# A macaron transformer layer on one core: masks in VectorE's maxima pass, low halves on GpSimd, half projections one step later

## The chip, the core and the metric

The program runs on one core of one Trainium2 chip. The metric is device time in microseconds (us), the median of several runs. TensorE (PE in the profile) multiplies matrices, VectorE (DVE), ScalarE (ACT) and GpSimd (POOL) work on elements, and SyncE (SP) issues the DMAs. Each engine has a queue of its own, run in order; between engines there are only semaphores.

## The reference, cut to what matters

32 samples of 512 tokens, width 256, 16 heads of 16, two of eight experts for each sample:

```python
x = x + 0.5 * ffn(layernorm(x))          # two experts of the sample, GELU
x = x + attention(layernorm(x))
x = x + 0.5 * ffn(layernorm(x))

# attention
q = cos * q + rotate_half(q) * sin
k = cos * k + rotate_half(k) * sin
scores = einsum('bhqd,bhkd->bhqk', q, k) / math.sqrt(DH)
scores = where(causal, scores, -inf)
out = einsum('bhqk,bhkd->bhqd', softmax(scores), v)
out = out.transpose(0, 2, 1, 3).reshape(b, t, d) @ Wo.T
```

## The kernel before

Three phases: feed-forward over all samples, attention over all samples, feed-forward again. The change is in attention, which fills the stretch from about 427 to 1900 us. Matrices are split into a high and a low half-precision part, so that a product takes three matmuls (`TERMS`).

**Slots and steps.** A sample s has four slots g = 0 to 3, one for each group of four heads; slots are counted through as G. Each slot has up to eleven steps n = 0 to 10. The order of every engine's work in a slot is written out by hand in that engine's `slot(s, g)`, and the queues follow it word for word.

**Work of a slot on TensorE.** At each step n it computes two things: with `scores` the transposed scores of the group two slots back (G - 2), with `max_scores` the scores of the present group, which serve only to find the maximum of each row. The first uses one half of the 128 rows of the array, the second the other half. Steps 0 to 3 of the maxima are one head's last 128 queries against all 512 keys, steps 4 to 7 one head against 384 keys, 8 and 9 two heads against 256, and 10 four heads against 128. Maxima scores go into three banks in turn (`MX_BANK`); a step waits until VectorE has read the bank. Scores go into two banks in turn; a step waits until ScalarE's exponential two steps back is done.

**The causal mask of the maxima.** In steps 0 to 3 VectorE adds the table `over` (f32, zero or -1e30) and takes the maximum in one custom pass (L996), followed by a read of its accumulator. In steps 4 to 10 TensorE adds the mask by one more matmul (L1167) and VectorE reduces (L1006).

**Rotation of the next sample.** In slots 0 and 1 TensorE projects q (tiles t = 0, 1) and k (t = 2, 3) of sample s + 1, each tile in two halves at steps 0, 1 and 4, 5. In slot 2 it projects v at the same steps. VectorE multiplies by the cosine (L974) and swaps neighbours (L975); GpSimd multiplies by the sine (L920, into `by_sin`) and adds (L924, into `rotated`, two buffers). ScalarE rounds to the high half (L1079, slots 1 and 2, steps 0 and 2), VectorE subtracts to get the low half (`rope_low`, L981, slots 1 and 2, steps 0 and 3: t = 0, 1 and t = 2, 3). Its semaphore is `qk_lo`.

**SP.** For sample s + 1: in slot 1 it waits for two low halves and writes the q image to memory (L879, two DMAs). In slot 2 it waits until that has landed, reads it back into the stacks in six DMAs (L846), waits for all four low halves and writes the k image (L888, two DMAs). In slot 3 it waits until this has landed, reads it into the stacks in six DMAs (L846) and waits until all twelve have landed. At the head of every slot it also waits for the negated maxima of the slot before and copies them into the stacks (L862); scores need them two slots later. `max_scores` at step 0 of slot 0 waits for both stacks.

**GpSimd.** In every slot it masks the exponentials of G - 2 with four selects (L912): the first behind exponential 4, two behind exponential 8, one behind 10. Between them stand the rotation of slots 0 and 1, and in slot 2 the power and the normalisation (L942, L948) of sample s + 2, for which TensorE's transposes at step 0 of slot 3 wait. The probabilities' products of the next slot wait for the masks.

```python
            if group(G - 2):
                pool.wait_ge(exp_done, 10 * (G - 2) + 4)
                mask(G, 0, probs[:, 0:4, 0:P], (4,))
            if g < 2 and sample(s + 1):
                rope(s + 1, 2 * g)
```

## Time and profile before

| what | us |
|---|---|
| median of 3 runs | 2292.76 |
| lowest, highest | 2287.46, 2299.47 |
| profiled execution, its own time | 2291.23 |
| its span, first to last instruction | 2289.5 |
| TensorE busy | 2109.5 (92%) |
| VectorE busy | 1931.8 (84%) |
| ScalarE busy | 1354.4 (59%) |
| GpSimd busy | 1306.6 (57%) |

The profile is one execution; its busy shares are means over three phases. In the attention phase the pattern of a sample repeats 32 times, so one sample of it, taken from the middle of the run (1017.8 to 1062.8 us), can be read instruction by instruction. A line such as L996 is a line of the kernel before; the granted TensorE clock is 0.989 of full speed over the span.

### The profile page before, as it was taken

What the parts mean: (1) busy time and instruction counts of PE and PEld (TensorE: products, weight loads), DVE (VectorE), ACT (ScalarE), POOL (GpSimd) and SP (SyncE); (2) the same over time, 40 slices, a digit from 0 to 9 for tenths busy, and PEclk for the clock granted to TensorE, in tenths of its full rate; (3) what the DMA queues carried; (4) which work ended last, traced back from release to release, by engine and by line L of the source; (5) the groups of instructions that cost most, each with busy time, mean ns of one, the idle gap of its engine ahead of it and who ended that gap; (6) DMA issues with size and microseconds to landing.
All of it is one profiled execution on the core that took longest, in us unless ns stands there. A gap on an engine that the chain in (4) does not pass through costs nothing.

```text
span 2289.5 us, 52899 instructions
## 1 busy us (share of the span) xinstructions
PE 2109.5 (92%) x17682; PEld 1141.4 (50%) x17682; DVE 1931.8 (84%) x4485; ACT 1354.4 (59%) x2568; POOL 1306.6 (57%) x1462
## 2 busy tenths in 40 slices
PE   4999999889999999999999999999999888999999
PEld 2666666434444444444444444444444434666666
DVE  6777788788999899999989998999999865777776
ACT  3455444266667666666666676666666655445553
POOL 6666667454555455456545554554555425666664
PEclk9999999899999999999999999999999999999999
DMA  6656666444445444444444454444445423666665
GB/s 208 192 192 207 201 203 200 116 89 89 98 95 101 94 94 98 89 94 93 99 89 100 95 101 94 96 92 96 93 94 98 99 70 118 197 202 194 204 207 167
DMA packets 280391, 295.29 MB, mean 129 GB/s; under 512 B 45784, under 2 KB 263224, under 8 KB 280120
## 3 DMA queue, kind: packets, MB, share of 16 engines
q1 hardware_dynamic: 280120, 291.90, 50.3%
q8 instruction: 143, 2.34, 0.5%
q14 instruction: 128, 1.05, 0.2%
HBM read 140.08 MB, written 83.89 MB: 98 GB/s over the span
## 4 chain that ended last, share of the span: by engine, by line
PE 45%; DVE 33%; SPq 7%; issue 6%; DMA 5%; ACT 4%; DVEq 0%; ACTq 0%
PE bank L710 8%; DVE bank L996 7%; DVE at_mx L1006 7%; PE bank L728 7%; PE bank L1185 6%; PE bank L1202 6%; PE bank L1219 4%; PE bank L1280 4%; ACT probs L1073 3%; DVE turned L975 3%; DVE v_qk L981 3%; DVE turned L974 2%; DVE at_stats L107 2%; PE bank L1255 2%; PE bank L1167 2%
## 5 line engine op out<-in xcount | busy, mean ns | idle before, releaser
L1073 ACT ACTIVATE probs<-bank 128x512 f32<-128x512 f32 x1280 | 747.0, 603 | 456.9 <-PE bank L1185 447.5
L912 POOL TENSOR_SCALAR_AFFINE_SELECT probs<-probs 128x512 f32<-128x512 f32 x512 | 320.4, 638 | 661.1 <-ACT probs L1073 659.3
L1006 DVE TENSOR_REDUCE at_mx<-bank 128x1 f32<-128x384 f32 (+2 forms) x896 | 509.6, 608 | 78.5 <-PE bank L1167 77.0
L1185 PE MATMUL bank<-stacks 49*128 49x512 f16 (+3 forms) x2048 | 458.7, 302 | 71.4 <-ACT probs L1073 71.0
L996 DVE CUSTOM_DVE_ANT_0 bank<-bank,xn 128x512 f32<-128x512 f32 x512 | 351.6, 698 | 38.8 <-PE bank L1158 36.2
L1185 PEld LDWEIGHTS bank<-stacks 49*128 49x128 f16 x2048 | 136.0, 94 | 458.6 <-ACT probs L1073 334.2
L1162 PE MATMUL bank<-stacks 48*128 48x384 f16 (+2 forms) x1536 | 307.7, 275 | 22.1 <-DVE at_mx L1006 15.6
L1167 PE MATMUL bank<-mask,turn 64*128 64x128 bf16 (+2 forms) x896 | 230.7, 257 | 0.0
L1158 PE MATMUL bank<-stacks 48*128 48x512 f16 x512 | 198.5, 389 | 10.6 <-DVE at_mx L996 6.4
L924 POOL TENSOR_TENSOR turned<-turned 128x512 f32<-128x512 f32 x128 | 184.7, 1443 | 19.1 <-POOL turned L920 0.4
L628 ACT ACTIVATE turned<-bank,b1s 128x512 f32<-128x512 f32 x128 | 88.2, 689 | 181.0 <-PE bank L710 179.3
L920 POOL TENSOR_TENSOR turned<-turned,at_sin 128x512 f32<-128x512 f32 x128 | 178.8, 1397 | 27.7 <-DVE turned L975 27.7
L628 ACT ACTIVATE probs<-bank,b1s 128x512 f32<-128x512 f32 x128 | 88.1, 688 | 178.9 <-PE bank L710 177.3
L710 PE MATMUL bank<-stacks 128*128 128x512 f16 x768 | 172.9, 382 | 19.3 <-DVE stacks L568 15.5
L728 PE MATMUL bank<-stacks,v_qk 128*128 128x256 f16 x1536 | 172.7, 273 | 0.0
L1202 PE MATMUL bank<-probs,v_qk 128*32 128x512 f32 (+3 forms) x2048 | 168.6, 448 | 0.0
L1202 PE MATMUL bank<-probs,v 128*32 128x512 f32 (+3 forms) x2048 | 164.3, 439 | 0.0
L728 PEld LDWEIGHTS bank<-stacks,v_qk 128*128 128x128 f16 x1536 | 150.3, 98 | 17.3
L1162 PEld LDWEIGHTS bank<-stacks 48*128 48x128 f16 x1536 | 110.7, 94 | 52.5 <-DVE at_mx L1006 27.0
L710 PEld LDWEIGHTS bank<-stacks 128*128 128x128 f16 x768 | 73.9, 98 | 108.9 <-DVE stacks L568 19.1
L483 POOL TENSOR_TENSOR f_rstd<-f_ve,minus_half 128x4 f32<-128x4 f32 x64 | 91.1, 1424 | 59.4 <-DVE f_ve L119 59.4
L710 PE MATMUL bank<-xThi,w1hi 128*128 128x512 f16 x256 | 99.1, 387 | 25.2 <-DVE xTlo L568 10.6
(145 smaller groups left out, 4619.6 us busy)
## 6 DMA issues: line engine op xcount, KB each, us to landing
stacks<-qk_image SPq DMA_DIRECT2D x384, 128.0 KB, 4.5
qk_image<-v_qk SPq DMA_DIRECT2D x128, 256.0 KB, 3.7
stacks<-w_hi SPq DMA_DIRECT2D x192, 128.0 KB, 3.7
stacks<-w_lo SPq DMA_DIRECT2D x192, 128.0 KB, 3.8
b2s<-in_b SPq DMA_DIRECT2D x128, 128.0 KB, 3.9
after_ffn<-probs SPq DMA_DIRECT2D x32, 512.0 KB, 6.5
at_x<-after_ffn SPq DMA_DIRECT2D x32, 512.0 KB, 4.1
late_x<-after_ffn SPq DMA_DIRECT2D x32, 512.0 KB, 4.7
```

What stands on the lines that cost most here:

```text
L710: ins = nc.tensor.matmul(h_ps[j][:], w, v, start=(n == 0), stop=(n == 3 * NC - 1))
L728: ins = nc.tensor.matmul(y_ps[t // 2][:, t % 2, :], v, w, start=(n == 0), stop=(n == 11))
L912: nc.gpsimd.affine_select(out=ap, in_=ap, compare_op=ALU.is_ge, fill=0.0, base=0, pattern=[[0, d] for d in dims] + [[1, P]], channel_multi ...
L924: nc.gpsimd.tensor_tensor(rotated[t % 2][:], by_cos[t % 2][:], by_sin[t % 2][:], ALU.add).then_inc(rope_done, 1)
L996: nc.vector.tensor_tensor_reduce(out=bank[:, 0:w], in0=bank[:, 0:w], in1=over[:, T - w:T], scale=1.0, scalar=LOWEST, op0=ALU.add, op1=ALU. ...
L1006: nc.vector.tensor_reduce(o_ap, i_ap, AX_X, ALU.max).then_inc(max_done, 1)
L1073: nc.scalar.activation(probs[:, c, :], st_ps[c % 2][:], ACT.Exp, scale=DH ** -0.5).then_inc(exp_done, 1)
L1158: nc.tensor.matmul(bank[:, 0:w], q_stack[s.par][rows, j + n % 4, i * P:(i + 1) * P], k_stack[s.par][rows, j + n % 4, 0:w], start=True, sto ...
L1162: nc.tensor.matmul(bank[:, at * w:at * w + w], q_stack[s.par][rows, j + a, i * P:(i + 1) * P], k_stack[s.par][rows, j + a, 0:w], start=(at ...
L1167: nc.tensor.matmul(last, tab.turn[const, :], over.broadcast_to([HP, nh, P]), start=False, stop=True).then_inc(mx_done, 1)
L1185: ins = nc.tensor.matmul(bank[:, col:col + T - q0], k_stack[ss.par][rows, j + ha, kt * P:(kt + 1) * P], q_stack[ss.par][rows, j + ha, q0:T ...
L1202: ins = nc.tensor.matmul(pv_ps[32 * a:32 * a + 32, kt * P:T], v[ss.par][:, kt, head_of(sg, a), :], p, start=(kt == 0), stop=(nth == 3), ti ...
```

## The change

1. The maxima of steps 4 to 7 lose their mask matmul on TensorE. VectorE adds the mask in its custom pass, as in steps 0 to 3, now for all eight one-head blocks.
2. `rope_low` moves from VectorE to GpSimd: t = 0 behind the first rotation of slot 1, t = 1 at that slot's end, t = 2 and 3 behind the first mask of slot 2, ahead of power and normalisation.
3. The sine product is written in place over the swapped tile, and the freed half of `turned` gives `rotated` four buffers (one for each t). The addition waits for `qk_lo` of three tiles back.
4. The second half of the projections at steps 4 and 5 comes at step 6, and so does the fourth tile of v.

```diff
-        rope = [[self.turned[:, 2 * j + i, :] for i in range(2)] for j in range(4)]
+        rope = [self.turned[:, 0:2, :], self.turned[:, 2:4, :], self.turned[:, 4:8, :]]
...
-            nc.gpsimd.tensor_tensor(by_sin[t % 2][:], swapped[t % 2][:], sin_t[:], ALU.mult).then_inc(sin_done, 1)
-
-            wait(pool, qk_lo, idx - 1)
+            nc.gpsimd.tensor_tensor(swapped[:, t % 2, :], swapped[:, t % 2, :], sin_t[:], ALU.mult).then_inc(sin_done, 1)
+
+            wait(pool, qk_lo, idx - 3)
             pool.wait_ge(sin_done, idx + 1)
-            nc.gpsimd.tensor_tensor(rotated[t % 2][:], by_cos[t % 2][:], by_sin[t % 2][:], ALU.add).then_inc(rope_done, 1)
+            nc.gpsimd.tensor_tensor(rotated[:, t, :], by_cos[:, t % 2, :], swapped[:, t % 2, :], ALU.add).then_inc(rope_done, 1)
+
+        def rope_low(n, t):
+            pool.wait_ge(qk_hi, 4 * n.b + t + 1)
+
+            wait(pool, q_written if t < 2 else k_written, 32 * n.b)
+            nc.gpsimd.tensor_tensor(qk.lo[:, t, :], rotated[:, t, :], qk.hi[:, t, :], ALU.subtract).then_inc(qk_lo, 1)
...
+            if g == 1 and sample(s + 1):
+                rope_low(s + 1, 0)
+            if g == 2 and sample(s + 1):
+                rope_low(s + 1, 2)
+                rope_low(s + 1, 3)
...
+            if g == 1 and sample(s + 1):
+                rope_low(s + 1, 1)
...
-        def rope_low(n, t):
-            dve.wait_ge(qk_hi, 4 * n.b + t + 1)
-
-            wait(dve, q_written if t < 2 else k_written, 32 * n.b)
-            nc.vector.tensor_tensor(qk.lo[:, t, :], rotated[t % 2][:], qk.hi[:, t, :], ALU.subtract).then_inc(qk_lo, 1)
...
-            if n < 4:
+            if n < 8:
                 i = 3 - n // 4
...
-                if g in (1, 2) and sample(s + 1) and n in (0, 3):
-                    rope_low(s + 1, 2 * (g - 1) + (n == 3))
...
-            if n < 4:
+            if n < 8:
                 nc.tensor.matmul(bank[:, 0:w], q_stack[s.par][rows, j + n % 4, i * P:(i + 1) * P],
...
-                if g < 2 and sample(s + 1) and n in (0, 1, 4, 5):
-                    project_qk(s + 1, 2 * g + (n > 3), half=(n in (1, 5)))
-                if g == 2 and sample(s + 1) and n in (0, 1, 4, 5):
-                    project_v(s + 1, (0, 1, 4, 5).index(n))
+                if g < 2 and sample(s + 1) and n in (0, 1, 4, 6):
+                    project_qk(s + 1, 2 * g + (n > 3), half=(n in (1, 6)))
+                if g == 2 and sample(s + 1) and n in (0, 1, 4, 6):
+                    project_v(s + 1, (0, 1, 4, 6).index(n))
```

GpSimd's queue from the first mask of slot 1 to the normalisation of slot 2, before:

```order
L912 AFFINE_SELECT probs<-probs 128x4x128
L920 TENSOR_TENSOR turned<-turned,at_sin 128x512
L924 TENSOR_TENSOR turned<-turned 128x512
L912 AFFINE_SELECT probs<-probs 128x4x128 x3
L920 TENSOR_TENSOR turned<-turned,at_sin 128x512
L924 TENSOR_TENSOR turned<-turned 128x512
L912 AFFINE_SELECT probs<-probs 128x4x128
L942 TENSOR_TENSOR at_rstd<-at_ve,minus_half 128x4
L948 TENSOR_SCALAR at_xn<-at_x,at_ve,at_rstd 128x256 x4
```

The same stretch of GpSimd's queue after the change (L930 is the low half, L953 and L959 the power and the normalisation):

```order
L912 AFFINE_SELECT probs<-probs 128x4x128
L920 TENSOR_TENSOR turned<-turned,at_sin 128x512
L924 TENSOR_TENSOR turned<-turned 128x512
L930 TENSOR_TENSOR v_qk<-turned,v_qk 128x512
L912 AFFINE_SELECT probs<-probs 128x4x128 x3
L920 TENSOR_TENSOR turned<-turned,at_sin 128x512
L924 TENSOR_TENSOR turned<-turned 128x512
L930 TENSOR_TENSOR v_qk<-turned,v_qk 128x512
L912 AFFINE_SELECT probs<-probs 128x4x128
L930 TENSOR_TENSOR v_qk<-turned,v_qk 128x512 x2
L953 TENSOR_TENSOR at_rstd<-at_ve,minus_half 128x4
L959 TENSOR_SCALAR at_xn<-at_x,at_ve,at_rstd 128x256 x4
```

Two low halves now stand in slot 1 and two more ahead of the power; the second closes the pair for which SP's first image write waits.

TensorE's queue in slot 0, from the turned output of step 5 to step 7, before (L1255 turns the output, L1219 is the half projection, L1185 and L1162 are scores and maxima, L1167 the mask):

```order
L1255 MATMUL bank<-ident,at_o 128x128 x4
L1219 MATMUL bank<-at_xThi,qkv_hi 128x512
L1219 MATMUL bank<-at_xThi,qkv_lo 128x512
L1219 MATMUL bank<-at_xTlo,qkv_hi 128x512
L1185 MATMUL bank<-stacks 128x384
L1185 MATMUL bank<-stacks 128x128
L1162 MATMUL bank<-stacks 128x384
L1167 MATMUL bank<-mask,turn 128x128
L1185 MATMUL bank<-stacks 128x384
L1185 MATMUL bank<-stacks 128x128
L1162 MATMUL bank<-stacks 128x384
L1167 MATMUL bank<-mask,turn 128x128
```

The same place after the change (L1258, L1222, L1188 and L1161 are those lines now):

```order
L1258 MATMUL bank<-ident,at_o 128x128 x4
L1188 MATMUL bank<-stacks 128x384
L1188 MATMUL bank<-stacks 128x128
L1161 MATMUL bank<-stacks 128x384
L1222 MATMUL bank<-at_xThi,qkv_hi 128x512
L1222 MATMUL bank<-at_xThi,qkv_lo 128x512
L1222 MATMUL bank<-at_xTlo,qkv_hi 128x512
L1188 MATMUL bank<-stacks 128x384
L1188 MATMUL bank<-stacks 128x128
L1161 MATMUL bank<-stacks 128x384
```

The half projection moved from ahead of step 6 to between steps 6 and 7, and the mask matmuls are gone.

## Rows read from the trace of the kernel before

**Rows 1.** page, part 1: busy time, share of the span, instructions of each engine

```profile
PE 2109.5 (92%) x17682; PEld 1141.4 (50%) x17682; DVE 1931.8 (84%) x4485; ACT 1354.4 (59%) x2568; POOL 1306.6 (57%) x1462
```

**Rows 2.** TensorE's timeline, one sample: start, us, engine line op out<-in [idle before <-releaser]

```profile
1017.81 0.39 PE L1158 MATMUL bank<-stacks 48*128 48x512 f16 x1
...
1024.85 0.22 PE L1185 MATMUL bank<-stacks 49*128 49x128 f16 x1
1024.86 0.22 PE L1167 MATMUL bank<-mask,turn 64*128 64x128 bf16 x1
...
1025.82 0.28 PE L1185 MATMUL bank<-stacks 49*128 49x256 f16 x1 [0.52 <-ACT probs L1073]
...
1038.47 0.39 PE L1162 MATMUL bank<-stacks 48*128 48x128 f16 x4 [0.41 <-DVE at_mx L1006]
...
1050.20 1.09 PE L1247 MATMUL bank<-ident,at_xn 128*128 128x128 f32 x8
...
1062.84 0.39 PE L1158 MATMUL bank<-stacks 48*128 48x512 f16 x1
```

**Rows 3.** groups by shape, 700 to 1700 us: line engine op | busy, mean ns | idle before

```profile
L996 DVE CUSTOM_DVE_ANT_0 bank<-bank,xn 128x512 f32<-128x512 f32 x356 | 244.6, 697 | 19.6 <-PE bank L1158 17.7
...
L1006 DVE TENSOR_REDUCE at_mx<-bank 128x1 f32<-128x384 f32 x354 | 187.3, 550 | 17.9 <-PE bank L1167 16.8
```

**Rows 4.** VectorE's timeline at the seam of slots 0 and 1

```profile
1028.52 0.69 DVE L1006 TENSOR_REDUCE at_mx<-bank 128x4 f32<-128x512 f32 x1
1029.12 0.69 DVE L996 CUSTOM_DVE_ANT_0 bank<-bank,xn 128x512 f32<-128x512 f32 x1
...
1029.73 1.19 DVE L981 TENSOR_TENSOR v_qk<-turned,v_qk 128x512 f16<-128x512 f32 x1
1030.84 0.68 DVE L996 CUSTOM_DVE_ANT_0 bank<-bank,xn 128x512 f32<-128x512 f32 x1
```

**Rows 5.** tile turned: duration ns min/median/max of each line's instructions

```profile
L920 POOL TENSOR_TENSOR turned<-turned,at_sin x128: 1262/1275/1785, 379.7 to 1805.1; 128x512 f32<-128x512 f32 x128
L924 POOL TENSOR_TENSOR turned<-turned x128: 1262/1280/1738, 381.0 to 1806.6; 128x512 f32<-128x512 f32 x128
```

**Rows 6.** GpSimd's timeline, slots 1 and 2 of the sample

```profile
1033.38 0.64 POOL L912 TENSOR_SCALAR_AFFINE_SELECT probs<-probs 128x512 f32<-128x512 f32 x1 [1.32 <-ACT probs L1073]
...
1037.14 1.22 POOL L912 TENSOR_SCALAR_AFFINE_SELECT probs<-probs 128x512 f32<-128x512 f32 x2
1038.81 0.64 POOL L912 TENSOR_SCALAR_AFFINE_SELECT probs<-probs 128x512 f32<-128x512 f32 x1 [0.45 <-ACT probs L1073]
1039.41 1.27 POOL L920 TENSOR_TENSOR turned<-turned,at_sin 128x512 f32<-128x512 f32 x1
1040.83 1.73 POOL L924 TENSOR_TENSOR turned<-turned 128x512 f32<-128x512 f32 x1
...
1044.94 1.02 POOL L942 TENSOR_TENSOR at_rstd<-at_ve,minus_half 128x4 f32<-128x4 f32 x1
1046.16 2.17 POOL L948 TENSOR_SCALAR at_xn<-at_x,at_ve,at_rstd 128x256 f32<-128x256 f32 x4 [0.20 <-issue]
```

**Rows 7.** SP's timeline of the sample: issue of its DMAs

```profile
1034.72 0.87 SPq L879 DMA_DIRECT2D qk_image<-v_qk  x2
...
1042.16 3.70 SPq L846 DMA_DIRECT2D stacks<-qk_image  x6
1046.19 0.89 SPq L888 DMA_DIRECT2D qk_image<-v_qk  x2
...
1053.17 2.90 SPq L846 DMA_DIRECT2D stacks<-qk_image  x6
```

**Rows 8.** landing of DMAs by line, L879 then L888; then SP's waits, 1050 to 1064

```profile
DMA to landing us min/median/max: 2.1/2.5/3.5
...
DMA to landing us min/median/max: 3.8/4.5/6.2
...
SPq L71 <- DMA stacks<-qk_image: 5.3, 1, 5.3
```

More of the change, by code:

```diff
@@ L759, in attention @@
     cos_t, sin_t = sb("cos", [P, T], F32), sb("sin", [P, T], F32)
-    q_stack, k_stack, v, qk, (swapped, by_cos, by_sin, rotated), ones = mem.of_attention()
+    q_stack, k_stack, v, qk, (swapped, by_cos, rotated), ones = mem.of_attention()
     x = mem.at_x
@@ L973, in begin_rope @@
             wait(dve, rope_done, idx - 1)
-            nc.vector.tensor_tensor(by_cos[t % 2][:], x_ps[t % 2][:], cos_t[:], ALU.mult)
-            nc.vector.stream_shuffle(swapped[t % 2][:], x_ps[t % 2][:], [i ^ 1 for i in range(32)]).then_inc(rope_in, 1)
-        def rope_low(n, t):
-            dve.wait_ge(qk_hi, 4 * n.b + t + 1)
-            wait(dve, q_written if t < 2 else k_written, 32 * n.b)
-            nc.vector.tensor_tensor(qk.lo[:, t, :], rotated[t % 2][:], qk.hi[:, t, :], ALU.subtract).then_inc(qk_lo, 1)
+            nc.vector.tensor_tensor(by_cos[:, t % 2, :], x_ps[t % 2][:], cos_t[:], ALU.mult)
+            nc.vector.stream_shuffle(swapped[:, t % 2, :], x_ps[t % 2][:], [i ^ 1 for i in range(32)]).then_inc(rope_in, 1)
         def maxima(s, g, n):
@@ L998, in maxima @@
                 return
-            if n < 8:
-                o_ap, i_ap = out[:, n - 4, 2:3], bank[:, 0:3 * P]
-            elif n < 10:
+            if n < 10:
                 a = 2 * (n - 8)
@@ L1078, in rope_high @@
             wait(act, q_written if t < 2 else k_written, 32 * n.b)
-            nc.scalar.activation(qk.hi[:, t, :], rotated[t % 2][:], ACT.Copy).then_inc(qk_hi, 1)
+            nc.scalar.activation(qk.hi[:, t, :], rotated[:, t, :], ACT.Copy).then_inc(qk_hi, 1)
         def high_of(hi, n, c, ps_done, hi_done):
```

## The prediction

> **Names.** A sample of attention is four slots (0 to 3) of eleven steps (0 to 10). T0 is the start of the step 0 maxima matmul in slot 0. It needs the stacks that SP's reads filled for that sample. T0 is at 1017.81 and next at 1062.84 us [rows 2], so a sample takes 45.03 us. Times below are often given as T0 plus something.
>
> **What bounds the kernel now.** I read the page's busy shares first: TensorE is busy 92% of the span, VectorE 84%, GpSimd 57% [rows 1]. That makes TensorE and VectorE the suspects and GpSimd look idle. The reader must not stop there, because the change gives GpSimd work whose place in its queue matters more than its sum.
>
> TensorE's timeline [rows 2]: it idles 0.52 us at step 8 in front of a scores pair, waiting for an exponential. There is one such gap per slot, four a sample. VectorE's maxima hold TensorE once more, 0.41 us at 1038.47. Without the three 0.52 that the change can reach and the 0.41, a sample would be 45.03 - 1.56 - 0.41 = 43.06 us. The moved half projection parts two score pairs, which costs an extra hand-over in each of three slots, between nothing and one 128-column matmul's 0.22 us; I take 0.15. So TensorE's own work bounds a sample near 43.5 us.
>
> **The change, part by part.**
>
> *Masks of steps 4 to 7 in VectorE's pass.* Each slot loses four mask matmuls of 0.22 us. They cost TensorE nothing: the mask starts at 1024.86 beside the 128-column scores matmul at 1024.85, in the other half of the array, and the scores matmul stays [rows 2]. What is gained is that the maximum can start some 0.06 us sooner. The Trainium skill, TensorE: Matmul & The Clock Gate, says that matmuls in distinct row groups run concurrently; by a sum that prices the 16 masks of a sample one after another (16 x 0.22) the change would free 3.5 us, and by the rows it frees none. On VectorE the 384-wide reduce (550 ns) becomes the custom pass, which the trace has only at 512 columns (697 ns) [rows 3]. At 512 the reduce holds VectorE for 0.60 us (1028.52 to 1029.12) and the pass with its accumulator read for 0.61 (1029.12 to 1029.73) [rows 4]. So the pass costs 0.01 more, 16 x 0.01 = 0.2 us per sample. Bounds: 0, and 16 x 0.08 = 1.3 us if the pass held the engine for its full 0.69. I take 0.2, as the timeline has it.
>
> *Low halves leave VectorE.* Four subtractions go. One holds VectorE 1.11 us (1029.73 to 1030.84), because GpSimd is in a two-input operation at that moment [rows 4]; the other three take about 0.6. That is 2.9 us per sample, 1.7 of it in slot 1, where VectorE has no idle time.
>
> *Half projection behind step 6.* TensorE now issues scores 6, then 0.65 us of projection, then scores 7, so exponential 6 is done when scores 8 come. The 0.52 us gap in slots 0, 1 and 2 closes. For slot 1 it is worth up to 0.52 us, and nothing if VectorE, which is busy through the end of slot 0, doesn't follow; I take 0.45, since the subtraction gone from slot 1 lets VectorE catch up. Slot 1's first mask on GpSimd moves from T0 + 15.57 (1033.38, [rows 6]) to T0 + 15.12.
>
> *Low halves arrive on GpSimd.* No trace row shows this subtraction there. Nearest rows: a GpSimd multiply or add of two 128x512 inputs, 1.27 us in the median and 1.79 at most [rows 5]. Below it the mask with one input, 0.64 [rows 6]. I take 1.27, pitch 1.30; bounds 0.64 and 1.79. The Trainium skill, GPSIMD Engine Reference, section 3.1, gives 4497 ns for 2048 elements and calls VectorE the place for elementwise work; a quarter would be 1.12 us, and four lows would then cost 0.6 us less than by the rows. The long ones should vanish: the add at 1040.83 is one, beside a subtraction of VectorE.
>
> Now the queue. Between slot 1's first mask and the end of the second low half GpSimd does: mask 0.60, sin 1.42 (1039.41 to 1040.83), add 1.30, **low 0** 1.30, two masks 1.22, mask 0.60, sin 1.42, add 1.30, **low 1** 1.30 [rows 6]. That is 10.46, all back to back, since the exponentials and rotations that they wait for come earlier. Low 1 ends at T0 + 25.58. Before, VectorE finished it at 1034.6, T0 + 16.8, just ahead of SP's first image write at 1034.72 [rows 7]. It is 8.8 us later.
>
> **Loop 1: GpSimd to the transposes.** Behind low 1: 0.15 wait, mask 0.60, lows 2 and 3 2.60, the power 1.22 (1044.94 to 1046.16), the four normalisations 2.17, 0.08 to TensorE. The transposes of the sample after next start at T0 + 25.58 + 6.82 = T0 + 32.40. Today they start at 1050.20 = T0 + 32.39 [rows 2, 6]. From there to the next T0 are 12.64 us of slot 3, in which nothing large changes. This loop gives 45.04: everything that TensorE and VectorE gained in slots 0 to 2 is waited away in front of the transposes.
>
> **Loop 2: SP's queue to the stacks.** SP does in order: write q image (behind low 1), maxima rows, read q into the stacks (six transfers, behind the written image), write k image, rows, read k (six, behind the written image), wait for all. Steps: low 1 to first issue 0.09, second issue 0.44, landing 2.5 [rows 8], 0.1: reads of q begin at T0 + 28.71 (now T0 + 24.35). The k image write is queued in the same DMA engines behind the reads of q: 1042.16 to 1046.19 + 0.45 + 4.5 = 8.98 us from the first read to landed [rows 7, 8]. Then 0.1, then k reads: 2.90 of issue and 5.3 of waiting, 8.2 [rows 7, 8]. Sum 28.71 + 8.98 + 0.1 + 8.2 = 45.99. Today reads of k begin at 1053.17 and land at 1061.4, 1.5 us ahead of T0: a slack that the 45.03 us hides. Ahead of that SP has two pauses, 1035.6 to before 1042.16 and 1047.1 to before 1053.17, in which it only waits for maxima rows [rows 7]. The later low 1 uses both up.
>
> The sample is as long as its longest loop: 46.0 (SP), 45.0 (GpSimd), 43.5 (TensorE). **So 45.03 becomes 45.99, 0.96 us more.** There are 31 such intervals; I count 30, as the last ones have the second layer's loads among them and no sample after them to prepare. 30 x 0.96 = 29 us. The lead-in, where sample 0's rotation runs beside the first feed-forward, moves two microseconds at most either way. The profiled execution took 2291.2 us (span 2289.5), and the median of the runs, 2292.8, is 1.5 above it. 2291.2 + 29 + 1.5 = 2321.
>
> **Rivals.**
>
> *Same (loop 2 is shorter).* The 8.98 holds a wait of SP for low 3 (from 1045.86 to 1046.19), and the k write took 3.8 to 6.2 us to land over the run [rows 8]. If it lands in 3.8, loop 2 is 45.3; without SP's wait, 45.0. Loop 1 then holds the sample at 45.0. Time 2281 to 2304. For: both bounds are close to today's; against: the DMA engines drain both transfers one behind the other, and issuing one earlier doesn't drain it earlier.
>
> *Faster.* Mechanism: the half-precision subtraction on GpSimd is cheap, at the 0.64 of the one-input row. Loop 1 is 2.6 us shorter, 42.4, and loop 2 is 1.3 shorter, 44.7, with 3.8 for the k write 44.0. It decides once loop 2 is under 44.6, and the sample can't fall below 43.5. At 43.75: 30 x -1.28 = -38, 2254 us (2245 to 2281). For: the 2.9 us off VectorE and 1.6 off TensorE are real. Against: both known two-input rows are 1.27.
>
> *Dearer lows.* At 1.79 each, loop 2 is 47.0 and loop 1 is 47.0: 30 x 2.0 = 60, 2353 us. A k write of 6.2 us would give as much. Against: with no two-input operation of VectorE from SBUF beside it, nothing in the rows makes 1.79. The Trainium skill, Advanced Engine Details and Errata, section VectorE Performance Modes, has GpSimd and VectorE block each other over the second port. By that rule the passes could block too; the trace shows no such pass: 512-wide ones take 697 ns in the mean [rows 3].
>
> **How the numbers follow.** Forecast (loop 2 between 45.4 and 46.6, 2304 to 2341 us): 0.52. Same: 0.20. Faster: 0.18. Dearer: 0.10. The likeliest is loop 2 at 46.0: 2321 us. The range 2275 to 2352 holds the forecast, same and half of dearer, with the nearest few hundredths of faster: 0.8. A measurement of this kernel can tell about 0.5% (11.5 us) from no change. Slower by more: 0.52 + 0.10 = 0.62. Within: 0.20. Faster: 0.18.
>
> **What the changed profile would show.** Interval between step 0 maxima matmuls of slot 0: 46.0. TensorE idle before that matmul, with the stacks' reads as releaser, about 1 us per sample, and a wait for GpSimd's normalisation in front of the transposes of slot 3, near 1 us. The 0.52 us gap at step 8 only in slot 3. GpSimd's lows 1.27 each, no 1.79 left, no idle time from slot 1's first mask to the normalisation. First image write of SP at T0 + 25.7, first k read at T0 + 37.8. VectorE's share down to about 80%. It is wrong if the lows take well under 1 us, if the k write lands within 8 us of the first q read, or if slot 1's first mask comes well before T0 + 15.

## The result, and the profile after

| kernel | median us | lowest to highest | runs | profiled execution, span |
|---|---|---|---|---|
| before | 2290.49 | 2287.46 to 2299.47 | 4 | 2291.2, 2289.5 |
| after | 2335.8 | 2331.36 to 2347.6 | 4 | 2331.36, 2329.6 |

After takes 1.0199 times the time of before (95% interval 1.0148 to 1.0251), 45 us more. The profiled executions are 40 us apart. The forecast was 2321 us, 2275 to 2352: the direction holds, the time is 15 us above it.

The page of after, its busy shares and its chain of waits by line:

```profile
PE 2141.1 (92%) x17170; PEld 1140.4 (49%) x17170; DVE 1910.9 (82%) x4869; ACT 1356.9 (58%) x2568; POOL 1406.5 (60%) x1590
...
DMA qk_image<-v_qk 10%; PE bank L710 8%; DMA stacks<-qk_image 7%; PE bank L728 6%; PE bank L1222 6%; PE bank L1205 6%; PE bank L1188 6%; SPq L846 6%; POOL turned L920 3%; POOL turned L924 3%; POOL probs L912 3%; POOL v_qk L930 2%; DVE f_pair L111 1%; ACT probs L1076 1%; PE bank L1161 1%
```

Against [rows 1] the shares of busy time hardly move. TensorE has 512 instructions fewer and is busy 32 us longer, the first hint that it ran slower somewhere. The chain is what changed: the image writes (`qk_image<-v_qk`), SP's reads (L846) and their landing (`stacks<-qk_image`) are now on it with 23%. The low half on GpSimd takes 1.16 us in the mean (L930), below the 1.27 that I took from the multiply (L920, 1.27 in after too).

TensorE's waits of after, 700 to 1700 us (total, times, longest):

```profile
PE bank L1161 <- DMA stacks<-qk_image: 26.4, 20, 2.3
PE bank L1161 <- DVE at_mx L1003: 23.8, 21, 1.1
PE bank L1188 <- ACT probs L1076: 13.0, 22, 0.6
...
PE bank L1250 <- POOL at_xn L959: 3.7, 19, 0.2
```

The first is the wait that the forecast named: 1.3 us in the mean, in front of nearly every sample. The third is the gap of 0.52 to 0.6 us at step 8, now once per sample instead of four times. The second was not foreseen: TensorE waits 1.1 us in each sample for a maximum of VectorE. The last is the wait for GpSimd's normalisation in front of the transposes. The forecast has it near 1 us; it is 0.2.

**Loop 2, step by step.** SP's and GpSimd's timelines of after, for the sample whose T0 is 990.07:

```profile
1016.89 1.18 SPq L879 DMA_DIRECT2D qk_image<-v_qk  x2
...
1020.31 2.69 SPq L846 DMA_DIRECT2D stacks<-qk_image  x6
1023.11 0.89 SPq L888 DMA_DIRECT2D qk_image<-v_qk  x2
...
1029.60 2.69 SPq L846 DMA_DIRECT2D stacks<-qk_image  x6
```

```profile
1006.83 0.64 POOL L912 TENSOR_SCALAR_AFFINE_SELECT probs<-probs 128x512 f32<-128x512 f32 x1 [1.80 <-ACT probs L1076]
1007.43 1.27 POOL L920 TENSOR_TENSOR turned<-turned,at_sin 128x512 f32<-128x512 f32 x1
1008.85 1.28 POOL L924 TENSOR_TENSOR turned<-turned 128x512 f32<-128x512 f32 x1
1010.08 1.17 POOL L930 TENSOR_TENSOR v_qk<-turned,v_qk 128x512 f16<-128x512 f32 x1
1011.19 1.82 POOL L912 TENSOR_SCALAR_AFFINE_SELECT probs<-probs 128x512 f32<-128x512 f32 x3
...
1015.64 1.16 POOL L930 TENSOR_TENSOR v_qk<-turned,v_qk 128x512 f16<-128x512 f32 x1
```

Slot 1's first mask is followed by everything the forecast listed, without a pause, up to low 1 at 1016.80, and SP's first image write starts 0.09 us behind it. (In this sample all of it comes some 1.55 us later than in most; it is one of the six in the table.) I took the same times from the two timelines in 29 samples of the run:

| step | forecast | after, median (lowest to highest) |
|---|---|---|
| T0 to slot 1's first mask | 15.12 | 15.21; 16.73 to 16.80 in six samples |
| T0 to the first image write | 25.67 | 25.28; 26.79 to 26.86 in those six |
| first write to first q read | 3.04 | 2.99 (2.99 to 3.50) |
| first q read to first k read | 9.08 | 9.32 (8.85 to 10.68) |
| first k read to the next T0 | 8.2 | 8.35 (7.7 to 9.0) |
| sum | 45.99 | 45.94 |

So the loop is as forecast; its mean is 46.33 in mid-run, mostly because of the six samples.

**What the six have.** TensorE's timeline at the start of one of them, and the granted clock (the last but two number of a window's row is the clock, 1.00 is 2.4 GHz and 0.50 is 1.2 GHz):

```profile
1037.61 0.37 PE L1161 MATMUL bank<-stacks 48*128 48x512 f16 x1 [1.30 <-DMA stacks<-qk_image]
...
1038.15 0.38 PE L1222 MATMUL bank<-at_xThi,qkv_lo 128*128 128x512 f16 x1
...
1039.45 0.63 PE L1222 MATMUL bank<-at_xThi,qkv_lo 128*128 128x512 f16 x1
```

```profile
1038.00:1040.00 2.00, 2.00 (x9) 0.58 (x9) 1.97 (x5) 0.74 (x2) 0.00 (x0) 0.80 0.00 0
1040.00:1042.00 2.00, 2.00 (x12) 0.50 (x14) 0.88 (x3) 0.60 (x1) 0.00 (x0) 0.50 0.18 57
```

The same 512-column matmul takes 0.38 us at 1038.15 and 0.63 at 1039.45. Ahead of this stretch TensorE had waited 1.30 us for the stacks. The clock is back at 1043. Everything behind it in slots 0 and 1 is some 1.55 us late, slot 1's first mask with it: a wait that loop 2 makes seems to lengthen loop 2 itself. This is read from the order of the two, no run tests it at this place, and 14 other waits there, of up to 2.33 us, have no such stretch behind them. Five more samples have one in slot 2, behind the wait for VectorE; their next T0 comes no later for it, as far as the table's steps show.

**Where the 40 us are.** By SP's store of each sample's output (L866): the first is at 525.55 before and 532.19 after, so the lead-in costs 6.6 us, and there the clock is 0.50 from 440 to 460 us where before had 0.76. The 28 intervals from there take 36.7 us more (46.35 each against 45.04), the last three 2.8 less, and what follows 0.4 less. Together 40.1.

**The wait for VectorE** (L1003) is at step 5 of slot 2. VectorE's timeline there, and GpSimd's beside it:

```profile
1062.88 0.41 DVE L111 TENSOR_TENSOR at_pair<-at_stats 128x4 f32<-128x4 f32 x1
1063.20 0.15 DVE L112 TENSOR_TENSOR at_pair<-at_stats 128x4 f32<-128x4 f32 x1
1063.28 1.12 DVE L113 TENSOR_TENSOR at_pair<-at_stats 128x4 f32<-128x4 f32 x1
1064.44 0.17 DVE L115 TENSOR_SCALAR at_ve<-at_pair 128x4 f32<-128x4 f32 x1
...
1064.79 0.47 DVE L119 SCALAR_TENSOR_TENSOR at_ve<-at_pair 128x4 f32<-128x4 f32 x1
```

```profile
1061.98 1.28 POOL L924 TENSOR_TENSOR turned<-turned 128x512 f32<-128x512 f32 x1
1063.22 1.16 POOL L930 TENSOR_TENSOR v_qk<-turned,v_qk 128x512 f16<-128x512 f32 x1
1064.58 0.67 POOL L912 TENSOR_SCALAR_AFFINE_SELECT probs<-probs 128x512 f32<-128x512 f32 x1 [0.20 <-ACT probs L1076]
```

Three operations of four elements per partition take 0.41, 1.12 and 0.47 us, and each ends within 0.03 us of an instruction of GpSimd (1063.26, 1064.38, 1065.25). L112 starts at the seam of two of GpSimd's instructions and L115 where GpSimd stands (1064.38 to 1064.58); neither is held. The tile's view over 700 to 1700 us says that this is so in every sample; before, then after:

```profile
L113 DVE TENSOR_TENSOR at_pair<-at_stats x22: 155/158/159, 728.3 to 1674.2; 128x4 f32<-128x4 f32 x22
```

```profile
L113 DVE TENSOR_TENSOR at_pair<-at_stats x21: 1119/1124/1126, 739.2 to 1668.7; 128x4 f32<-128x4 f32 x21
```

The statistics thus cost VectorE 1.5 us more per sample (0.25 + 0.97 + 0.31), and TensorE waits 1.13 us for the maximum behind them. In after I take this to have cover, since the next T0 waits for the stacks anyway; no run removes this wait alone. The Trainium skill, GPSIMD Engine Reference, section 1 (Specifications), has GpSimd's interfaces to SBUF shared with VectorE, with contention for VectorE instructions in a two-port mode or with two inputs in SBUF. The trace agrees for those with two inputs (1.12 us where before has 0.16), and it adds that even a mask of GpSimd with one input holds them.

### The profile page after: what moved, and what is told of

It reads as the page before. It is cut to its first block, busy times and chain, and to the rows that moved or that the text cites. A ratio compares the mean times of both kernels' runs of the same rounds, so it can differ in the third digit from the quotient of the medians.

```text
span 2329.6 us, 52385 instructions
## 1 busy us (share of the span) xinstructions
PE 2141.1 (92%) x17170; PEld 1140.4 (49%) x17170; DVE 1910.9 (82%) x4869; ACT 1356.9 (58%) x2568; POOL 1406.5 (60%) x1590
## 4 chain that ended last, share of the span: by engine, by line
PE 39%; DMA 22%; SPq 13%; POOL 11%; DVE 7%; issue 6%; ACT 2%; POOLq 0%; DVEq 0%; ACTq 0%
DMA qk_image<-v_qk 10%; PE bank L710 8%; DMA stacks<-qk_image 7%; PE bank L728 6%; PE bank L1222 6%; PE bank L1205 6%; PE bank L1188 6%; SPq L846 6%; POOL turned L920 3%; POOL turned L924 3%; POOL probs L912 3%; POOL v_qk L930 2%; DVE f_pair L111 1%; ACT probs L1076 1%; PE bank L1161 1%
## 5 line engine op out<-in xcount | busy, mean ns | idle before, releaser
L1003 DVE CUSTOM_DVE_ANT_0 bank<-bank,xn 128x512 f32<-128x512 f32 (+1 forms) x1024 | 627.5, 640 | 130.2 <-PE bank L1161 129.3
L1188 PE MATMUL bank<-stacks 49*128 49x512 f16 (+3 forms) x2048 | 462.9, 304 | 24.7 <-ACT probs L1076 24.2
L1161 PE MATMUL bank<-stacks 48*128 48x512 f16 (+1 forms) x1024 | 352.7, 366 | 78.2 <-DMA stacks<-qk_image 41.4
L1188 PEld LDWEIGHTS bank<-stacks 49*128 49x128 f16 x2048 | 136.8, 94 | 404.2 <-ACT probs L1076 275.5
L1011 DVE TENSOR_REDUCE at_mx<-bank 128x2 f32<-128x512 f32 (+1 forms) x384 | 247.6, 687 | 44.0 <-PE bank L1170 44.0
L920 POOL TENSOR_TENSOR turned<-turned,at_sin 128x512 f32<-128x512 f32 x128 | 163.0, 1274 | 33.1 <-DVE turned L988 33.1
L924 POOL TENSOR_TENSOR turned<-turned 128x512 f32<-128x512 f32 x128 | 163.8, 1280 | 19.0 <-POOL turned L920 0.4
L1165 PE MATMUL bank<-stacks 48*128 48x256 f16 (+1 forms) x1024 | 149.4, 248 | 2.4 <-DVE at_mx L1003 0.5
L930 POOL TENSOR_TENSOR v_qk<-turned,v_qk 128x512 f16<-128x512 f32 x128 | 147.1, 1159 | 0.0
L1003 DVE DVE_READ_ACCUMULATOR2_ANT at_mx<- 128x1 f32 x1024 | 145.9, 142 | 0.0
L1161 PEld LDWEIGHTS bank<-stacks 48*128 48x128 f16 x1024 | 85.6, 93 | 118.6 <-issue 53.1
```

Of the source, the lines that this page charges most:

```text
L920: nc.gpsimd.tensor_tensor(swapped[:, t % 2, :], swapped[:, t % 2, :], sin_t[:], ALU.mult).then_inc(sin_done, 1)
L924: nc.gpsimd.tensor_tensor(rotated[:, t, :], by_cos[:, t % 2, :], swapped[:, t % 2, :], ALU.add).then_inc(rope_done, 1)
L930: nc.gpsimd.tensor_tensor(qk.lo[:, t, :], rotated[:, t, :], qk.hi[:, t, :], ALU.subtract).then_inc(qk_lo, 1)
L1003: nc.vector.tensor_tensor_reduce(out=bank[:, 0:w], in0=bank[:, 0:w], in1=over[:, T - w:T], scale=1.0, scalar=LOWEST, op0=ALU.add, op1=ALU. ...
L1011: nc.vector.tensor_reduce(o_ap, i_ap, AX_X, ALU.max).then_inc(max_done, 1)
L1161: nc.tensor.matmul(bank[:, 0:w], q_stack[s.par][rows, j + n % 4, i * P:(i + 1) * P], k_stack[s.par][rows, j + n % 4, 0:w], start=True, sto ...
```

## The experiments

Each was timed beside the kernel before (medians 2289 to 2291 us). "Sample" is the mean distance of SP's output stores in mid-run. The expectations call the forecast's account **theory A**: the sample is as long as the longest of SP's loop, GpSimd's loop and TensorE's own 43.5 us. **Theory D** was formed after the first four runs: the half projection at step 6 lets TensorE run ahead until it has to wait for VectorE in slot 2, and the clock falls behind that wait. Of D, the wait and the fall of the clock behind it are in the traces; that TensorE's lead makes the wait is not borne out (see f_half_only).

| label | median us | ratio (95%) | sample us |
|---|---|---|---|
| after | 2335.8 | 1.0199 (1.0148 to 1.0251) | 46.33 |
| e_low1_early | 2309.44 | 1.0082 (1.0056 to 1.0109) | 45.40 |
| e_norm_first | 2328.19 | 1.0151 (1.0121 to 1.0181) | 45.80 |
| e_both | 2284.91 | 0.9981 (0.9965 to 0.9998) | 44.62 |
| e_low_dve | 2338.69 | 1.0207 (1.0181 to 1.0233) | 46.61 |
| f_masks_only | 2295.02 | 1.0010 (0.9987 to 1.0033) | 45.06 |
| f_half_only | 2336.17 | 1.0194 (1.0151 to 1.0237) | 46.51 |
| f_lows_only | 2340.3 | 1.0210 (1.0167 to 1.0253) | 46.38 |
| f_low_dve_stats3 | 2353.75 | 1.0266 (1.0223 to 1.0310) | 47.22 |
| g_half_busy | 2319.19 | 1.0113 (1.0077 to 1.0149) | 45.69 |
| g_half_qk | 2368.64 | 1.0338 (1.0308 to 1.0369) | 47.64 |
| g_both_tuned | 2265.37 | 0.9883 (0.9851 to 0.9916) | 43.93 |

### The two loops, each taken away

**e_low1_early**: after, with low 1 ahead of two masks and of the next rotation, right behind low 0. GpSimd's work stays the same; only loop 2 starts sooner.

```diff
             if g == 1 and sample(s + 1):
                 rope_low(s + 1, 0)
+                rope_low(s + 1, 1)
...
-            if g == 1 and sample(s + 1):
-                rope_low(s + 1, 1)
```

> The changed kernel, with low 1 moved on GpSimd from the end of slot 1 to right behind low 0 (all else, and the sum of GpSimd's work, as in the changed kernel). Theory A (SP's image loop sets the sample): low 1 ends some 4.5 us earlier in the sample, the loop falls from 46.3 us to about 42, and GpSimd's loop to the transposes takes over at 44.6: about 2279 us (2268 to 2291), and TensorE's wait for the stacks is gone. Theory B (GpSimd's loop of masks, lows and normalisation sets it): nothing changes, 2330 to 2345. Theory C (the wider custom passes or the moved half projection cost it): nothing changes, 2330 to 2345.

The wait for the stacks is gone and with it the half clock (the windows show 1.00 over 700 to 1700 us). The sample is 45.4 and steady. TensorE's waits show why it isn't shorter:

```profile
PE bank L1187 <- ACT probs L1075: 36.2, 44, 1.1
PE bank L1249 <- POOL at_xn L960: 28.0, 22, 1.3
```

The second is GpSimd's normalisation in front of the transposes, 1.3 us in each of 22 samples. It is where the forecast had loop 1, but not loop 1 as forecast, in which GpSimd never stands. Here GpSimd stands in front of slot 2's first mask:

```profile
1006.31 0.64 POOL L912 TENSOR_SCALAR_AFFINE_SELECT probs<-probs 128x512 f32<-128x512 f32 x1 [1.32 <-ACT probs L1075]
```

The moved low 1 makes the rotation behind it 1.1 us later. ScalarE's fourth high half waits 1.91 us for that rotation, and the exponential behind it, which this mask needs, is late. TensorE waits for an exponential behind that high half, too, 1.0 to 1.1 us (in the first line above). The transposes start at T0 + 32.77 in the median, in after at T0 + 31.69; with the 12.64 of slot 3 behind them that is 45.4. So that SP's loop was the longest is shown; the expected 2279 us (2268 to 2291) was missed, because the move itself makes a new loop through GpSimd and ScalarE.

VectorE's timeline here also shows that one input doesn't keep an operation from being held:

```profile
1003.86 1.16 DVE L115 TENSOR_SCALAR at_ve<-at_pair 128x4 f32<-128x4 f32 x1
```

It starts inside an add of GpSimd (1003.73 to 1004.99) and ends 0.03 us behind it.

**e_norm_first**: after, with lows 2 and 3 behind the normalisation, which shortens loop 1 alone.

```diff
-            if g == 2 and sample(s + 1):
-                rope_low(s + 1, 2)
-                rope_low(s + 1, 3)
...
+            if g == 2 and sample(s + 1):
+                rope_low(s + 1, 2)
+                rope_low(s + 1, 3)
```

(The second place is behind `normalise` and ahead of the next masks.)

> The changed kernel, with lows 2 and 3 moved on GpSimd from ahead of the power and normalisation to behind them; low 1 stays at the end of slot 1. Theory A (SP's image loop): the normalisation comes 2.3 us earlier and TensorE's wait in front of the transposes goes, but the stacks come no sooner: 2325 to 2345 us, with a longer wait for the stacks at slot 0. Theory B (GpSimd's loop): 30 samples shorter by 1.5 to 2 us, 2275 to 2295. Theory C: as the changed kernel.

As A has it, the wait for the stacks stays, though it is not longer, as expected, but a little shorter:

```profile
PE bank L1161 <- DMA stacks<-qk_image: 22.8, 20, 1.7
```

Only 8 us of the total come back, but 0.5 us of each sample. SP issues the k write 0.8 us later than in after, its second DMA lands in 5.0 us instead of 5.9 (medians of 26 samples), and the k reads behind it land sooner too; no run shows why. In the profiled execution the last three samples take 15 us more than in after, with a stretch of 48 us at half clock, and hide most of that gain.

**e_both**: both moves.

> Both moves of the two kernels before together: low 1 behind low 0, lows 2 and 3 behind the normalisation. Theory A with GpSimd's loop as the next bound: both loops are under TensorE's and VectorE's own work, a sample of 43.5 to 44.3 us, 2246 to 2270 us. Theory B: the same as with the normalisation first alone. Theory C: no faster than 2320.

Both waits are gone (but for one of 0.9 us for the stacks), and the kernel is level with before, a little faster (0.9981). The sample of 44.62 is still 1.1 above the 43.5 that A leaves, so A missed a wait here. It is at step 5 of slot 2; TensorE's timeline, then ScalarE's:

```profile
1039.06 0.33 PE L1187 MATMUL bank<-stacks 49*128 49x384 f16 x1 [1.04 <-ACT probs L1075]
```

```profile
1037.89 0.63 ACT L1081 ACTIVATE v_qk<-turned 128x512 f16<-128x512 f32 x1 [1.91 <-POOL turned L924]
1038.42 0.58 ACT L1075 ACTIVATE probs<-bank 128x512 f32<-128x512 f32 x1
```

ScalarE has the fourth high half (L1081) queued at step 2 of slot 2, ahead of exponentials. With low 1 moved up, GpSimd ends that rotation later, ScalarE stands 1.91 us, and the exponential behind it comes too late for TensorE, as in e_low1_early. No half clock follows this wait of 1.04.

### The parts alone

**e_low_dve**: after, with the low halves on VectorE again (same places as before); masks in the pass, half projection and the four-deep tile stay.

```diff
-            if g == 1 and sample(s + 1):
-                rope_low(s + 1, 0)
...
+                if g in (1, 2) and sample(s + 1) and n in (0, 3):
+                    rope_low(s + 1, 2 * (g - 1) + (n == 3))
```

> The changed kernel with all four low halves back on VectorE at steps 0 and 3 of slots 1 and 2; masks in VectorE's pass, half projections at step 6 and the four-deep rotated tile stay. Theory A: the loop of SP is as in the kernel before, and only what TensorE gains at step 8 shows, as far as VectorE (bound in slot 1) lets it: 2265 to 2290 us. Theory C (passes or half projection): still 2310 or more.

This refuted A as the whole explanation. Both of its loops are undone, and the kernel is as slow as after. TensorE's timeline has a wait in slot 2 that A has no name for:

```profile
1017.65 0.33 PE L1156 MATMUL bank<-stacks 48*128 48x384 f16 x1 [1.57 <-DVE at_mx L996]
```

D was formed here: of the parts left, only the half projection moves TensorE. The trace has one thing more: VectorE's low half ahead of that wait takes 1.63 us here, in every sample of mid-run (0.69 in before).

**f_masks_only**: before, with the masks of steps 4 to 7 in VectorE's pass.

```diff
-            if n < 4:
+            if n < 8:
```

> The kernel before with one part of the change: the masks of steps 4 to 7 in VectorE's pass. Theory D (in the kernel with the lows back on VectorE, 2338.7 us, the loss comes from TensorE running ahead through the moved half projection into a longer wait for VectorE in slot 2, after which its granted clock falls to half): this part alone leaves TensorE's lead alone, 2284 to 2296 us, no stretch at half clock. Theory C1 (the wider pass costs VectorE 0.1 us or more each, 1.6 us a sample): 2320 to 2345.

1.0010 (0.9987 to 1.0033), sample 45.06: sixteen mask matmuls fewer per sample, and nothing gained or lost, as the forecast said.

**f_half_only**: before, with the half projection at step 6.

```diff
-                if g < 2 and sample(s + 1) and n in (0, 1, 4, 5):
+                if g < 2 and sample(s + 1) and n in (0, 1, 4, 6):
...
-                if g == 2 and sample(s + 1) and n in (0, 1, 4, 5):
+                if g == 2 and sample(s + 1) and n in (0, 1, 4, 6):
```

> The kernel before with one part of the change: the half projection (and fourth tile of v) at step 6. Theory D: TensorE is 0.5 us earlier per slot while VectorE, bound in slot 1, is not, so its wait in slot 2 at step 5 (0.18 us before) passes 1 us and the granted clock falls for some 3.5 us of the sample: 2320 to 2345 us. Rival (the moved projection pays off as costed): 30 x -0.5 to -1.0 us, 2260 to 2278.

The move alone costs 45 us, in the range that D gave. TensorE's timeline and the windows behind it:

```profile
1015.25 0.33 PE L1162 MATMUL bank<-stacks 48*128 48x384 f16 x1 [1.59 <-DVE at_mx L996]
```

```profile
1013.00:1015.00 2.00, 0.66 (x6) 0.17 (x3) 1.90 (x9) 2.00 (x6) 1.03 (x2) 1.00 1.16 128
...
1017.00:1019.00 2.00, 2.00 (x14) 0.87 (x12) 1.81 (x5) 0.67 (x2) 1.42 (x3) 0.50 1.08 216
```

TensorE is busy 0.66 of 2 us, waiting for VectorE; from 1016.7 its 256-column matmuls take 0.42 us instead of 0.27, at a clock of 0.50. VectorE is busy 1.90 of the same 2 us. It is late because of GpSimd: the low half takes 1.67 us, and an operation of four elements 0.62 beside a mask of GpSimd at 1013.18. VectorE's timeline, then GpSimd's:

```profile
1009.58 1.67 DVE L981 TENSOR_TENSOR v_qk<-turned,v_qk 128x512 f16<-128x512 f32 x1
...
1013.21 0.62 DVE L111 TENSOR_TENSOR at_pair<-at_stats 128x4 f32<-128x4 f32 x1
```

```profile
1009.43 1.27 POOL L924 TENSOR_TENSOR turned<-turned 128x512 f32<-128x512 f32 x1
```

GpSimd's add starts 0.15 us ahead of the low half, and the low half ends 0.55 us behind the add's end. In before the two start the other way round: the low half comes first, here beside the add that starts at 1040.83 [rows 6], takes its usual 0.69 us, and the add is the one that is held (1.73):

```profile
1040.73 0.69 DVE L981 TENSOR_TENSOR v_qk<-turned,v_qk 128x512 f16<-128x512 f32 x1
```

**The sample that decides.** One sample of f_half_only (850.16 to 894.39) has the old order. GpSimd stands there 0.44 us between its multiply and its add, once in the run, and so comes second. VectorE's low half, GpSimd's add, and the sample's window:

```profile
872.62 0.68 DVE L981 TENSOR_TENSOR v_qk<-turned,v_qk 128x512 f16<-128x512 f32 x1
```

```profile
872.75 1.68 POOL L924 TENSOR_TENSOR turned<-turned 128x512 f32<-128x512 f32 x1 [0.44 <-POOL turned L920]
```

```profile
850.16:894.39 44.23, 42.43 (x394) 19.33 (x394) 41.15 (x101) 30.35 (x60) 24.17 (x29) 1.00 0.48 97
```

TensorE has the same lead (slot 2 starts at T0 + 20.8 in both), but waits 0.18 us at step 5 as in before, instead of 1.59, the clock stays, and the sample takes 44.23 us: 0.80 less than before, between the 0.5 and 1.0 that I had as the rival for this kernel. In g_half_qk the corresponding sample has the low half at 0.68 too and takes 44.57 us. So the lead alone costs nothing. The move shifts VectorE and GpSimd against each other by some 0.25 us, and the low half that now comes second makes the wait. No run sets this order on purpose; the two samples show it.

**f_lows_only**: before, with the low halves on GpSimd, the sine in place and four rotated tiles (this part of the diff as it stands above).

> The kernel before with one part of the change: the low halves on GpSimd with the in-place sine and the four-deep tile; masks and projections as before. Theory A (SP's image loop): slot 1's first mask stays at T0 + 15.6, so the loop is 0.3 to 0.5 us longer than in the changed kernel if nothing else held that one up; with TensorE's own pace unchanged 46.3 to 46.8 us a sample, 2325 to 2345. Rival (the loss of the changed kernel is from the other two parts): 2270 to 2290, as VectorE has 2.9 us less to do.

A's mechanism alone also costs as much as the whole change: the 28 samples take 36 us more than in before, in after 37. Of the 50 us of the total, 11 are in the last three samples, where 48 us on end run at half clock in the profiled execution. The wait for the stacks is there:

```profile
PE bank L1163 <- DMA stacks<-qk_image: 17.3, 20, 2.4
```

Each part is enough by itself, and the two are not added: 2336, 2340, and 2336 with both. With both, VectorE has no low half that could be held, and what TensorE gains or loses in slot 2 would be waited away at the next T0 in any case. This last is argued, not shown.

### The clock or VectorE

**f_low_dve_stats3**: e_low_dve, with the statistics behind step 3 of slot 2 instead of step 1, to get them out of GpSimd's way.

```diff
-                if g == 2 and sample(s + 2) and n == 1:
+                if g == 2 and sample(s + 2) and n == 3:
```

> The kernel with the low halves back on VectorE (2338.7 us), and the statistics of the sample after next moved in slot 2 from behind step 1 to behind step 3. Theory D: VectorE's pass of step 2 comes 2.2 to 2.7 us sooner, TensorE's wait at step 5 (1.57 us) and the stretch at half clock behind it go: 2265 to 2290 us. Rival (the passes themselves, or the projection's place, cost it): 2325 or more.

Missed. The statistics are no longer held (L111 165 ns in the median, L113 158), but the kernel is slower still, with samples of 45.4, 47.0 and 48.5 us. The low half is still held, 1.63 us in every sample, VectorE's work has moved to another place where TensorE waits for it (0.9 and 0.7 us), and the clock is down for longer (0.66 in the mean from 1020 to 1030 us).

So freeing the statistics is not enough; this run left the larger of the two holds in place. The samples of this kernel sort by their mean clock without exception: 45.4 us at 1.00, 47.0 at 0.96, 48.5 at 0.93. That is a step of about 1.5 us for each further stretch at 1.2 GHz.

**g_half_busy**: f_half_only, with twelve discarded matmuls of 256 columns where TensorE waits in slot 2. They compute nothing that is used; VectorE's work is the same.

```diff
+                if g == 2 and sample(s + 1) and n == 5:
+                    for _ in range(12):
+                        nc.tensor.matmul(x_ps[1][:, D:2 * D], xT.hi[:, 0, 3 * P:4 * P], tab.qkv.hi[:, 0, 2 * D:3 * D], start=True, stop=True)
```

> The kernel before with the half projection at step 6 (2336 us), and twelve extra 256-column matmuls, whose results are overwritten unused, in TensorE's queue at step 5 of slot 2, between the scores and the maxima, where it waits 1.6 us for VectorE. Theory E (not the wait but the half clock behind it costs the time): the wait becomes busy time, the granted clock stays at 2.4 GHz, and the sample falls from 46.5 us to 45.0 or less: 2275 to 2295 us. Rival (the wait itself, or VectorE's slowed operations, cost it): the extra matmuls change nothing or add their 1.3 us: 2330 to 2375.

Adding work to TensorE makes the kernel 17 us faster: 2336.2 to 2319.2. That lies between the two ranges that I had given. In the profiled executions the 28 samples take 25 us less, and the last three 15 more, with 48 us on end at half clock. The row of the whole stretch, f_half_only and then g_half_busy:

```profile
700.00:1700.00 1000.00, 934.16 (x8458) 423.03 (x8450) 916.32 (x2169) 649.95 (x1289) 519.82 (x621) 0.98 0.45 92
```

```profile
700.00:1700.00 1000.00, 960.92 (x8847) 448.63 (x8849) 932.31 (x2214) 663.78 (x1315) 532.29 (x635) 1.00 0.45 94
```

The clock stays at 1.00, and the sample falls from 46.51 to 45.69. In f_half_only itself the samples come in two kinds, and the short kind has the same 45.7. Two neighbours of it:

```profile
990.12:1037.20 47.08, 43.96 (x400) 19.85 (x396) 42.78 (x102) 30.22 (x61) 24.29 (x29) 0.96 0.45 91
1037.20:1082.88 45.68, 42.47 (x400) 19.39 (x396) 42.59 (x102) 30.25 (x61) 24.27 (x29) 1.00 0.44 94
```

47.1 us at a mean clock of 0.96, 45.7 at 1.00, and so through the run, but for the one of 44.23. So the low clock costs 0.8 us of each sample's 1.5, as a mean over both kinds, and the filler takes back just that. The other 0.65 us are in the kernel without any low clock: 0.80 gained by the move, and 1.45 lost in TensorE's wait for the held VectorE (45.68 against 44.23), which the filler covers with work that brings nothing. I expected 45.0, so this share I had not foreseen.

**g_half_qk**: before, with only the half projections of slots 0 and 1 at step 6; those of v stay at step 5.

```diff
-                if g < 2 and sample(s + 1) and n in (0, 1, 4, 5):
-                    project_qk(s + 1, 2 * g + (n > 3), half=(n in (1, 5)))
+                if g < 2 and sample(s + 1) and n in (0, 1, 4, 6):
+                    project_qk(s + 1, 2 * g + (n > 3), half=(n in (1, 6)))
```

> The kernel before with the half projections of slots 0 and 1 at step 6; the fourth tile of v stays at step 5 of slot 2. Theory D (TensorE's lead comes from slots 0 and 1; VectorE meets GpSimd's rotation in slot 2 and is late for step 5): the wait of 1.6 us and the half clock stay, 2325 to 2345 us. Rival (the new place in slot 2 itself costs it, since step 5 is no longer covered by the v tile): 2275 to 2292.

The wait stays, so the moves in slots 0 and 1 are enough to make it; the low half takes 1.67 us here too. The wait is as long as in f_half_only (32.0 us in 21 times there), but the size of the loss was outside what D gave. Its samples go by clock: 46.0 us at 1.00 (44.57 with the low half not held), 47.2 to 47.7 at 0.96, 48.7 at 0.93 and 50.2 at 0.90. There are more stretches at half clock; why isn't shown.

```profile
PE bank L1162 <- DVE at_mx L996: 32.1, 21, 1.6
```

### A version that beats both

**g_both_tuned**: e_both, with ScalarE's fourth high half at step 5 of slot 2 instead of step 2, and VectorE's statistics behind step 2 instead of step 1.

```diff
-                if g == 2 and sample(s + 2) and n == 1:
+                if g == 2 and sample(s + 2) and n == 2:
...
-                if g in (1, 2) and sample(s + 1) and n in (0, 2):
-                    rope_high(s + 1, 2 * (g - 1) + (n == 2))
+                if g in (1, 2) and sample(s + 1) and n in (0, 2 if g == 1 else 5):
+                    rope_high(s + 1, 2 * (g - 1) + (n > 0))
```

> The kernel with low 1 behind low 0 and lows 2 and 3 behind the normalisation (2285 us), with two more moves in slot 2: ScalarE's fourth high half from step 2 to step 5 (TensorE waits 1.04 us at step 5 for the exponential behind it) and the statistics from behind step 1 to behind step 2 of VectorE's queue. If the exponential's wait is what holds slot 2: 0.4 to 0.9 us a sample less, 2258 to 2273 us. If another wait takes its place (the step 3 pass, half clock): 2280 to 2330.

```profile
PE bank L1187 <- ACT probs L1075: 18.2, 44, 0.6
PE bank L1160 <- DVE at_mx L1002: 8.8, 23, 0.4
PE bank L1160 <- DMA stacks<-qk_image: 3.0, 5, 0.9
...
700.00:1700.00 1000.00, 966.00 (x8573) 438.20 (x8570) 914.20 (x2579) 687.37 (x1369) 629.97 (x755) 1.00 0.46 98
```

2265.37 us, 0.9883 of before (0.9851 to 0.9916). TensorE is busy 966 of 1000 us at full clock, and most samples take 43.7 us. The forecast put TensorE's own work near 43.5; 1.3 us of waits per sample are still in its samples, as its 43.5 had a gap left in slot 3. The two last moves were made together, so what each brings isn't shown. All parts of the change are in this kernel. Four pieces of work stand in other places than in after: low 1, lows 2 and 3, one high half and the statistics.

## Why the forecast was right, and where not

- **Loop 2 (SP's queue) decides at 45.99**: right. Its steps sum to 45.94 in the median, and e_low1_early, which moves low 1 alone, takes the wait away.
- **Low half 1.27 us, pitch 1.30**: mis-sized. It takes 1.16, one follows another in 1.11, and the first image write comes 0.4 us sooner for it.
- **k image written 8.98 us behind the first q read**: mis-sized the other way. The k write lands in 5.7 us in the median (4.1 to 7.4) against 4.5 in [rows 8], and the step is 9.32 from first read to first read. The two errors nearly cancel, so that 45.99 is closer than its terms.
- **Loop 1 (GpSimd) at 45.04**: 0.7 us too long, for the same reason. In after the transposes start at T0 + 31.69 in the median, not 32.40, which gives 44.3, and the expected wait of 1 us for the normalisation is 0.2. The 45.4 of e_low1_early is another loop, which goes through ScalarE. Loop 2 decides all the same.
- **TensorE's own work near 43.5**: near; 43.7 in g_both_tuned.
- **Masks free nothing, and the wider pass costs 0.01 each**: right within what can be measured (f_masks_only). The 384-wide pass takes 578 ns where the reduce of [rows 3] took 550.
- **The half projection gains 0.5 us a slot and costs nothing**: true only while VectorE's low half stays ahead of GpSimd's add. In the one sample of f_half_only where it does, the sample takes 44.23 us, 0.8 below before. In the others of mid-run it comes second, takes 1.67 us instead of 0.69, and TensorE waits 1.6 us and then often runs at half clock: alone, the move costs 45 us. The forecast had this hold in its rows (1.11 us for one low half, [rows 4]), but moved the engines without asking which of the two would now come first. In after the low halves are off VectorE, and what is left of it is hidden behind loop 2. A forecast for this part alone would have been wrong in sign.
- **The long operations vanish with VectorE's subtraction**: true of GpSimd's (none of the 1.7 us kind is left), but the contention moved to VectorE's small statistics operations, 0.16 to 1.12 us. I had looked for it only in the passes.
- **30 x 0.96 = 29 us, lead-in within 2 us**: the clock was left out, and this is the larger part of the miss. The profiled executions are 40 us apart instead of 29. Stretches at 1.2 GHz cost 1.55 us in each of six samples, some 9 us; without them the 28 intervals are 0.98 longer each, as forecast. The lead-in's 6.6 us go with 12 us more at half clock there. The last three samples and the rest give back 3, where the forecast had 2 more. The remaining 3 us or so of the 15 are that the median of after is 4.4 above its profiled execution; the forecast took 1.5. So the time is closer than its terms, by some luck.
- **Rivals**: "same" needed a k write of 3.8 us; its median rose instead. "Faster" needed a subtraction at 0.64; it takes 1.16. "Dearer lows" is out by the same number; and its remark that a k write of 6.2 us would give as much is a slip, since 1.7 us more make loop 2 47.7, some 2372 us.
- **Open**: why the clock falls behind one wait and not behind another. It fell behind the wait of 0.9 us of f_low_dve_stats3 and behind waits of 1.13 to 1.82 us in after, and not behind the 1.04 of e_both or the 1.27 of e_low1_early. Within after, six samples have it at T0, and others with waits of up to 2.33 us there have not. The same wait of 1.13 us in slot 2 is followed by it at 1065.98 and not at 1018.40. The runs show that it follows waits of TensorE, not which of them. Open too is why the last samples of some kernels run at half clock for 48 us on end (f_lows_only, e_norm_first, g_half_busy).

## What to carry to other kernels

Price a moved instruction by where it ends in each queue's loop from one repetition to the next, and take the longest loop; then ask the same for every part alone, since a part that only closes TensorE's gaps also shifts the other engines against each other. Here 0.15 us in the order of one instruction of VectorE and one of GpSimd decide over 1.45 us of each sample. One odd sample among equal ones is worth a look for such an order. An operation moved to a half idle engine is paid by whoever stands behind it there: here the places of a few instructions in three queues were worth 70 us, from 2336 to 2265, at equal work. Where TensorE waits near a microsecond or more, read the granted clock just behind the wait.

## What the hardware showed that I had not expected

- VectorE's operations on 128x4 elements in SBUF take 0.16 us alone, and up to 1.16 us while GpSimd is in an instruction: they end when it ends, within 0.03 us. A mask of GpSimd with one input does it too (0.62 us beside it), and an operation of VectorE with one input is held like the others (1.16 us in e_low1_early). Those that start within 0.02 us of GpSimd's own start are not held (L112 and L117 in after, 0.15 and 0.16).
- Of a two-input operation of VectorE and one of GpSimd that overlap, the one that starts second is held: 0.69 and 1.73 us with VectorE first by 0.10 us, 1.67 and 1.27 with GpSimd first by 0.15.
- In f_half_only TensorE is busy 93% of the time, and the granted clock still falls to 1.2 GHz for some 3 us in two samples of three. One such stretch costs 1.2 to 1.6 us (45.84 to 47.05 in e_low_dve, 45.43 to 47.05 in f_low_dve_stats3). Twelve useless matmuls in a wait gave 17 us back.
- A half-precision result of a two-input subtraction with single-precision and half-precision inputs costs GpSimd 1.16 us at 128x512; single precision throughout costs 1.27.
